# Attention on one core: sums from spare columns, reciprocals two steps later, projections as fp32r splits, TensorE's loop written out

## The reference, cut to what matters

```python
q = (x @ Wq + bq).reshape(B, N, H, d).transpose(0, 2, 1, 3)
k = (x @ Wk + bk).reshape(B, N, H, d).transpose(0, 2, 1, 3)
v = (x @ Wv + bv).reshape(B, N, H, d).transpose(0, 2, 1, 3)
scores = jnp.einsum('bhqd,bhkd->bhqk', q, k) * SCALE
allowed = jnp.abs(idx[:, None] - idx[None, :]) <= half        # half = 64
attn = jax.nn.softmax(jnp.where(allowed, scores, -jnp.inf), axis=-1)
out = jnp.einsum('bhqk,bhkd->bhqd', attn, v)
return out.transpose(0, 2, 1, 3).reshape(B, N, D) @ Wo + bo
...
h = h + attention(layernorm(h))
```

## Time and profile before

| | us |
|---|---|
| median of 3 runs (lowest, highest) | 2761.98 (2761.46, 2766.01) |
| profiled execution, its own time | 2763.8 |
| its span | 2762.1 |
| attention phase, by the windows | about 415 to 1160 |
| TensorE busy over the span | 2544.0 (92%) |
| DVE busy over the span | 1870.7 (68%) |
| mean granted TensorE clock | 0.953 |

### The profile page before, as it was taken

One profiled execution on the slowest core, in us unless ns is written; L12 is line 12 of the kernel. 1 busy time (PEld: TensorE's weight loads), 2 busy tenths in 40 slices (PEclk: granted clock), 3 DMA queues, 4 the chain that ended last, 5 costly groups with the idle time before them and its releaser, 6 DMA issues.

```text
span 2762.1 us, 52306 instructions
## 1 busy us (share of the span) xinstructions
PE 2544.0 (92%) x21673; PEld 2308.9 (84%) x21673; DVE 1870.7 (68%) x2148; ACT 1354.8 (49%) x1292; POOL 242.1 (9%) x147
## 2 busy tenths in 40 slices
PE   8959985898889889559999999999999999999999
PEld 6736684776667667459999999999999999999999
DVE  7849913655556566386766767666877777777774
ACT  2238801322223223255353443537977777777771
POOL 2202201000000000031121212100000000000000
PEclk9989996988989999879999999999999999999999
DMA  3435513000000000000000000003000000000000
GB/s 113 128 90 148 139 33 136 10 17 9 17 9 17 14 12 13 14 12 24 17 27 23 17 23 17 23 28 115 28 20 23 24 20 21 25 20 20 27 16 9
DMA packets 83907, 103.44 MB, mean 37 GB/s; under 512 B 8919, under 2 KB 75111, under 8 KB 83047
## 3 DMA queue, kind: packets, MB, share of 16 engines
q1 hardware_dynamic: 80167, 90.99, 10.9%
q0 software_dynamic: 3616, 10.54, 1.5%
HBM read 71.14 MB, written 30.36 MB: 37 GB/s over the span
## 4 chain that ended last, share of the span: by engine, by line
PE 56%; DVE 1%; issue 0%; DMA 0%; POOL 0%; ACT 0%; SPq 0%; POOLq 0%; DVEq 0%
PE spline_acc L1620 31%; PE spline_acc L1603 8%; PE spline_acc L1602 8%; PE spline_acc L1604 8%; PE spline_xT L1583 0%; DMA spline_x<-h_scr 0%; DVE spline_weights_low L1327 0%; DVE spline_xn L569 0%; DVE spline_f L1360 0%; DVE spline_t L1348 0%; DVE spline_b L1343 0%; DVE spline_b L1337 0%; DVE spline_a L1332 0%; POOL spline_rstd L1299 0%; ACT spline_a L1491 0%
## 5 line engine op out<-in xcount | busy, mean ns | idle before, releaser
L1620 PE MATMUL spline_acc<-spline_weights,spline_f 128*128 128x192 f32 x5248 | 853.0, 326 | 0.0
L1620 PEld LDWEIGHTS spline_acc<-spline_weights,spline_f 128*128 128x128 f32 x5248 | 852.8, 190 | 0.0
L1368 DVE SCALAR_TENSOR_TENSOR spline_f<-spline_n,spline_b 128x2048 f32<-128x2048 f32 x164 | 376.0, 2293 | 183.7 <-PE spline_acc L1620 181.9
L1602 PE MATMUL spline_acc<-spline_f,spline_weights_high 128*128 128x328 f32 x1536 | 479.8, 312 | 7.2 <-DVE spline_f L1360 7.2
L1603 PE MATMUL spline_acc<-spline_f,spline_weights_high 128*128 128x328 f32 x1536 | 482.4, 314 | 0.0
L1604 PE MATMUL spline_acc<-spline_f,spline_weights_low 128*128 128x328 f32 x1536 | 476.2, 310 | 0.0
L1602 PEld LDWEIGHTS spline_acc<-spline_f,spline_weights_high 128*128 128x128 f32 x1536 | 289.9, 189 | 7.4 <-issue 7.4
L1603 PEld LDWEIGHTS spline_acc<-spline_f,spline_weights_high 128*128 128x128 f32 x1536 | 289.1, 188 | 0.0
L1604 PEld LDWEIGHTS spline_acc<-spline_f,spline_weights_low 128*128 128x128 f32 x1536 | 288.7, 188 | 0.0
L1360 DVE SCALAR_TENSOR_TENSOR spline_f<-spline_n,spline_a 128x984 fp32r<-128x984 f32 x128 | 151.1, 1180 | 200.1 <-PE spline_acc L1604 198.4
L912 ACT ACTIVATE attend_probs<-scores_by_key 82x1968 f32<-82x1968 f32 x64 | 115.7, 1807 | 316.2 <-PE scores_by_key L1040 316.2
(11 more groups left out here) (154 smaller groups left out, 3567.3 us busy)
## 6 DMA issues: line engine op xcount, KB each, us to landing
sample_pos<-pos_scr SPq DMA_DIRECT2D x32, 540.0 KB, 4.4
hid_scr<-spline_hid SPq DMA_DIRECT2D x64, 164.0 KB, 1.8
spline_xn<-hid_scr SPq DMA_DIRECT2D x41, 256.0 KB, 3.1
pix_scr<-stem_by_pixel SPq DMA_DIRECT2D x32, 225.0 KB, 2.5
sample_h<-pix_scr POOLq DMA_DIRECT2D x32, 225.0 KB, 4.4
spline_weights_raw<-w SPq DMA_DIRECT2D x1, 6144.0 KB, 22.0
spline_weights<-w SPq DMA_DIRECT2D x4, 1536.0 KB, 6.1
h_scr<-attend_h SPq DMA_DIRECT2D x16, 246.0 KB
```

What stands on the lines that cost most here:

```text
L1368: nc.vector.scalar_tensor_tensor(f2[i][:], n_[u][:], MAGIC + i, b_[u][:], ALU.is_equal, ALU.mult).then_inc(f_ready, 1)
L1602: nc.tensor.matmul(z, high, x_high, start=start, stop=False)
L1620: last = nc.tensor.matmul(z, f2[i][:, r * P:(r + 1) * P], w2[:, i, r, :], start=(i == 0 and r == 0), stop=(i == 3 and r == 4 * CH - 1))
```

## The change

The edits, in the order of the diff:

1. The ones of the sums move into `va`: its spare columns 16 to 31 of each head are set to 1.0, so one `mix` gives results and sums. The second pass against `ones` is gone. The step's output is copied to SBUF by ACT (`mix_out`, to `mixed[i]`).
2. The sums (rows 16, 48, 80, 112) go to DRAM, come back as 48x41, are inverted by DVE in the step after (`invert`, behind part q = 2 of the maxima), go to DRAM again and come back broadcast to 32 rows each, in four DMAs. DVE weighs at the start of the second step after (`weigh`), and `project_out` takes the image of two steps back. SP does nothing else.
3. Loads of x and stores of h move from SP to POOL, and the residual is loaded from DRAM instead of computed from x; `bo` enters through a sum row of `wo`.
4. q, k and v are each five fp32r matmuls where there were two float32 ones: x is split by ACT (`turned`, three copies) and DVE (`low_x`), the weights once at the start.
5. Window pieces and masks are fp32r instead of bf16, with even widths.
6. Values are copied out of PSUM by ACT instead of DVE.
7. TensorE's order: in the second step `mix` is in two parts, one behind `values` and one behind part q = 3; in the first step the k projections come last. `project_out` moves from behind part 1 to behind part 0.
8. TensorE's loop is written out; the other engines keep theirs.

```diff
-            def load(t, u):
-                sp.dma_start(even[0:VIS], vis[:, b, :]).then_inc(x_in[u], 16)
...
+            def invert(t, i):
+                sp.wait_ge(mix_ready, 2 * t + i + 1)
+                sp.dma_start(total_scr[i], mixed[i][DH:P:32, :]).then_inc(total_out[i], 16)
+                sp.wait_ge(total_out[i], 16 * t + 16)
+                sp.dma_start(total[i][0:SUMS, :], total_scr[i].rearrange("j (k n) -> (j k) n", n=PART)
+                             ).then_inc(total_in[i], 16)
+                sp.wait_ge(inverted, 2 * t + i + 1)
+                sp.dma_start(rec_scr[i].rearrange("j (k n) -> (j k) n", n=PART), rec[i][0:SUMS, :]
+                             ).then_inc(rec_out[i], 16)
+                sp.wait_ge(rec_out[i], 16 * t + 16)
+                for j in range(4):
+                    sp.dma_start(spread[i][32 * j:32 * j + 32, :],
...
+            def pair(tt, u, more=True):
                 t = 2 * tt + u
                 pool.wait_ge(ln, LN_STEPS * t + LN_VAR)
                 pool.tensor_tensor(rstd[0:ROWS, :], ve[0:ROWS, :], minus_half[0:ROWS, :], ALU.pow).then_inc(pow_done, 1)
                 if not (isinstance(tt, int) and tt == 0):
-                    pool.wait_ge(h_ready, 2 * t - 2)
-                pool.tensor_tensor(resid[u][0:ROWS], x[u][0:ROWS],
-                                   bo[0:ROWS, :, :].to_broadcast([ROWS, 4, D]), ALU.add).then_inc(resid_ready, 1)
+                    leave(t - 2, u)
+                load(pool, resid[u], resid_in[u], t)
+                if more:
+                    pool.wait_ge(xn_ready, t + 1)
+                    load(pool, x[u], x_in[u], t + 2)
...
+                    if not first:
+                        weigh(t - 1, i)
                     for q in range(4):
                         if i == 0 or more:
                             maximum(nxt, q)
+                        if q == 0:
+                            if i == 0 and more:
+                                for j in range(2):
+                                    low_x(t + 1, j, use(t, X[j]))
+                            if not first:
+                                residual(tt - 1 if u == 0 else tt, v, i, use(t, Y[i]))
+                            if i == 1 and more2:
+                                norm_in(tt + 1, u)
+                        if q == 1 and i == 1 and more2:
+                            norm_out(tt + 1, u, use(t, X[1]))
...
-                nc.tensor.matmul(xb[:, bank, 0:PT], w[0:D0, 0, g, :], xT[0:D0, 0, :], start=True, stop=False)
-                nc.tensor.matmul(xb[:, bank, 0:PT], w[0:D1 + 1, 1, g, :], xT[0:D1 + 1, 1, :],
-                                 start=False, stop=True).then_inc(filled[bank], 1)
+                nc.tensor.matmul(y, high[:, 0, c], xh[:], start=True, stop=False)
+                nc.tensor.matmul(y, high[:, 0, c], xl[:], start=False, stop=False)
+                nc.tensor.matmul(y, low[:, 0, c], xh[:], start=False, stop=False)
+                nc.tensor.matmul(y, high[:, 1, c], xr[:], start=False, stop=False)
+                nc.tensor.matmul(y, low[0:D1 + 2, 1, c], xe[0:D1 + 2, :], start=False,
+                                 stop=True).then_inc(filled[bank], 1)
...
-            with pe.Fori(1, PAIRS // 2 - 1) as tt:
+            for tt in range(1, PAIRS // 2 - 1):
                 for u in range(2):
                     pair(tt, u)
```

More of the change, by code:

```diff
@@ L870, in _ @@
                 low_k(0, g, start(START["K"][g]), HG + g + 1)
-            for i in range(2):
-                values(0, i, start(START["V"][i]))
             for q in range(4):
@@ L913, in expo, with pair @@
                                      ACT.Exp, scale=SCALE).then_inc(exped, 1)
-            def pair(tt, u, more=True):
+            def pair(tt, u, first=False, more=True):
                 t = 2 * tt + u
@@ L941, in _ @@
                 high(k1[0][:, g, :], start(START["K"][g]))
+            act.wait_ge(zeros_set, 5)
+            for i in range(2):
+                values(0, i, start(START["V"][i]))
             high(mh[:], start(START["MAX"]))
-            for u in range(2):
-                pair(0, u)
+            pair(0, 0, first=True)
+            pair(0, 1)
             with act.Fori(1, PAIRS // 2 - 1) as tt:
@@ L1097, in pair @@
-                        if q == 2 and more:
+                        if q == 0:
+                            if i == 0 and more:
+                                for j in range(2):
+                                    turn_x(t + 1, j, use(t, X[j]))
+                            if not first:
+                                project_out(a - 2, i, use(t, Y[i]))
+                        if q == 2:
                             if i == 0:
-                                read(use(t, X[0]), use(t, X[1]))
-                                for g in range(2):
-                                    project(wq, g, use(t, Q[g]))
-                            else:
-                                values(0, use(t, V[0]))
@@ L1104, in pair @@
-                    if i == 0 and more:
-                        project(wq, 2, use(t, Q[2]))
-                    pe.wait_ge(exped, 2 * a + 2)
-                    mix(u, i, use(t, SUM[i]), True)
+                                if more:
+                                    read(use(t, X[0]), use(t, X[1]))
+                                    for g in range(2):
+                                        project(wqh, wql, g, use(t, Q[g]))
+                            else:
+                                if more:
+                                    values(0, use(t, V[0]))
+                                mix(a, u, i, 0, use(t, MIX[i]))
@@ new lines, in pair @@
+                    if i == 0:
+                        if more:
+                            project(wqh, wql, 2, use(t, Q[2]))
+                        read(*(start(START["V"][j]) if first else use(t - 1, V[j]) for j in range(2)))
+                        for c in range(2):
+                            mix(a, u, i, c, use(t, MIX[i]))
+                    else:
+                        mix(a, u, i, 1, use(t, MIX[i]))
+                        if more:
+                            values(1, use(t, V[1]))
@@ L1108, in pair @@
                     if nxt:
                         turn_max(a + 1, use(t, MAX[i]))
-                    if more:
-                        if i == 0:
-                            for g in range(HG):
-                                project(wk, g, use(t, K_[g]))
-                        else:
-                            values(1, use(t, V[1]))
-                    if i == 0:
-                        read(*(start(START["V"][j]) if first else use(t - 1, V[j]) for j in range(2)))
-                    mix(u, i, use(t, MIX[i]), False)
+                    if i == 0 and more:
+                        for g in range(HG):
+                            project(wkh, wkl, g, use(t, K_[g]))
```

326 lines of the change are left out of this document (178 added, 148 removed).

## The result

The changed kernel takes 2850.7 us (median of 4 runs, 2848.9 to 2854.3) against 2761.7 for the kernel before (4 runs, 2754.8 to 2766.0): ratio 1.0326, 95% interval 1.0302 to 1.0350. It is 89 us slower where 22 faster was forecast, and outside the range.

The account below looks back on a forecast made before the run. TensorE was taken to set the pace; twelve pairs at 44.1 - 43.0 gave 13.2 us, with 3.5, 2.4, -2.3, 13.3 and -6.3 a sum of 23.8: 2763.8 - 23.8 = 2740.0 us, range 2645 to 2797.

Parts of the forecast that it names:

- What goes: Attention savings: a 1.8 us mix per step, projections 0.74 for 1.21 us, values 0.9, loop return 7.3, DVE reciprocals, SP's loads.
- The k wait: First step's end: with k projections last, the next step's scores wait the full 1.3 us for the last k.
- The loop's return: TensorE's loop in attention: writing it out saves 48.0 - 40.7 = 7.3 us, in five or six pairs.
- The second step: Second step of a pair: 12.4 us of work, part 2 of queries waits 1.6, part 3 waits 0.5, 14.5 in all.
- The wait for POOL: DVE waits for POOL's power behind seven DMA issues: 7y - 1.9 us, a stall of 3.4 per pair, ends 1.8 and 7.2.
- y: One DMA issue on POOL in attention, taken at 0.75 us from earlier rows of 0.53 to 1.30.
- the slow rival: POOL becomes the bound: each 0.1 us per issue costs 9 us in all; at 1.30 the result is 2790; chance 0.25.
- The clock after the stall: TensorE at half clock behind the DVE wait: 4.0 us, ends 1.6 in all and 8; second step's drop another 1.6.
- The round trip of the reciprocals: DMAs between DVE's reciprocal and weighing, about 5 us, costed at nothing; bound 3 us per landing, 2.9 us late per pair.
- the quick rival: POOL issues at 0.53 us: stall 1.8, clock holds, 5.6 us less per pair, 2667 us; chance 0.30.
- late reciprocals: Rival: landings take 3 us, DVE weighs 2.9 us late per pair, pair 38 us, 2778; chance 0.05.
- The ends: Outside the twelve pairs: gains 3.5 and 2.4 ahead; after, -2.3, 13.3 from last half pairs, -6.3 at the end.

Follow-up runs that it names:

- the waits gone: Changed kernel with all loads and stores on SP and transfers cut to 80 and 2 rows, TensorE's loop kept: 2724.0 us, 37.5 more than written out.
- rows split: Transfers cut to 80 and 2, 32 and 14, 32 and 4 rows: changed kernel with loads and stores on SP 2686.5 us, changed kernel itself 2817.4 us.
- the norm earlier: Changed kernel with loads and stores on SP, transfers cut to 80 and 2 rows, and DVE's norm_in ahead of the second step's first maximum: 2639.9 us.
- the power first: Changed kernel with POOL computing a pair's power before issuing the seven DMAs, not behind them: 2836.8 us, ratio 1.0260.
- the corner without either cause: Changed kernel with POOL's power ahead of its DMAs and transfers cut to 80 and 2, 32 and 14, 32 and 4 rows: 2719.4 us.

## Why the prediction was wrong

**Where the miss lies.** The profiled execution took 2848.9 us where 2740.0 was forecast. Of these 109 us, 63 lie in the twelve pairs (48.3 us each for 43.0), 22 ahead of them and 24 behind them.

**What goes: nearly right.** Five fp32r matmuls of a projection take 0.86 us where 0.74 was forecast: those behind the first follow at 0.15 us, as rows 1 gave, but the first takes 0.26 (timeline of PE, changed kernel; the next group starts at 826.83):

```profile
825.97 0.42 PE L1039 MATMUL attend_spare<-attend_x_high,attend_wk_high 128*128 128x328 f32 x1 [0.48 <-ACT attend_mixed L954]
826.23 0.31 PE L1040 MATMUL attend_spare<-attend_x_low,attend_wk_high 128*128 128x328 f32 x1
...
826.83 0.40 PE L1039 MATMUL attend_spare<-attend_x_high,attend_wk_high 128*128 128x328 f32 x1
...
830.19 0.70 PE L1093 MATMUL scores_by_key<-attend_q,attend_k 32*82 32x164 f32 x24 [1.11 <-issue]
```

The k wait is the last row, 1.1 us for 1.3. The loop's return was worth what rows 2 said, in the kernel before (39) and with the waits gone (37.5); where another wait held the pair it was worth 25. A pair without the stall and at full clock was forecast at 34.0 us; with rows split, such a pair (721.6 to 757.1, granted clock 1.00) takes 35.5. The 1.5 us too little lie mostly in the projections (0.1 each) and in `project_out`, which waits 2.27 us there for its bank where I took 1.2. That the twelve pairs with the norm earlier average 35.6, the forecast's 34.0 + 1.6, is luck: their wait of part 2 is nearly gone, which the forecast had in it, and their mean clock is 0.92. The second step had the right wait in it (part 2 behind the norm, 1.6; measured 1.76).

**The wait for POOL: right mechanism, one issue mis-sized.** y, one issue on POOL, was taken at 0.75 and is 1.19 in the mean; 7y - 1.9 would then give 6.4, and DVE's wait is 7.1. The rows from which y came span it (0.53 to 1.30), but I took the value of one short-row transfer for seven that move 72 to 328 rows. The row of 0.53 was not undisturbed either, as the prediction has it: a DVE operation of 3.16 us (L414, from 192.55) runs over it. The figure of about 1 us in the Trainium skill, "DMA: Bandwidth & Descriptors", section "Latency and other measured facts", lay nearer to the measured 1.19 than mine. By the slow rival's own formula 1.19 gives 2740 + 7 x 0.44 x 13 = 2780. That is still 71 us short.

**The clock after the stall: too small.** I took 4.0 + 1.6 us with an upper end of 8. The stall is 6.45 us on TensorE, not 4, and the clock stays at 0.50 from 793 to 814: 7.0 us. From part 2 of the queries at 790.71 to that of the next pair at 838.16 TensorE waits 10.45 us in all, where the pair at full clock above waits 5.92 (it has no wait ahead of part 3, but 2.27 instead of 0.52 for `low_x`). So this pair comes out as 35.5 + 4.5 + 7.0 = 47.0, of 47.5 measured; the mean of the twelve is 48.3.

**The round trip of the reciprocals at nothing: the step that failed.** Landings were taken from rows 8, of other phases, and the bound was 3 us; `rec_scr` takes 5.0 us beside the loads (6.5 with the power first). In this kernel that is partly hidden by the stall for POOL (2.05 us of waiting at 809.51 in the pair shown), which is why the forecast's own suspect looked like the whole answer. It still costs 33 us here, 20 of them in the twelve pairs (559.8 us with rows split for 579.5), though DVE's wait for the power is longer with rows split. And it carries as much as POOL does: had y been 0.53, I estimate that the quick rival would have got not 2667 but something near 2837, the power-first kernel, in which DVE hardly waits for the power. I gave late reciprocals 0.05, and named them in the last line as what would make the forecast wrong. In the power-first kernel they do, by 117 us against the corner without either cause.

**The ends.** To the fourth power the forecast gained 5.9 us and the changed kernel loses 15.9. The first power alone comes 8.5 us later (439.43 for 430.90; with rows split 432.43), and in the fourth period DVE already waits 7.33 us for the power, which the sum left out. From the sixteenth power on, the forecast gained 4.7 us (-2.3 + 13.3 - 6.3); the changed kernel loses 19.2. The last three `project_out` that wait are these (timeline of PE):

```profile
1186.17 4.11 PE L1135 MATMUL attend_spare<-attend_wo,attend_oT 128*82 128x192 f32 x12 [6.95 <-DVE attend_oT L839]
...
1219.56 3.84 PE L1135 MATMUL attend_spare<-attend_wo,attend_oT 128*82 128x192 f32 x12 [8.64 <-DVE attend_oT L839]
1230.27 3.62 PE L1135 MATMUL attend_spare<-attend_wo,attend_oT 128*82 128x192 f32 x12 [6.86 <-DVE attend_oT L839]
```

I had one such wait, at the very end. With rows split this stretch gains 7.8 us (89.1 for 96.9), and the start, to the fourth power, 7.9 where 5.9 were forecast. That kernel has its moves on SP, so this shows that the two ends can be had, not that each piece was sized rightly.

**Open.** How the rows of a transfer are dealt to the 16 DMA engines isn't in the profile; that 82 rows land in 11 us and 80 in 2.6 is shown, and the busy share of 0.13 points to two engines, but no other cut of 82 (41 + 41, 64 + 18) was tried. Whether 46 and 36 rows are slow by themselves is not shown either: they were always in flight behind the store of h, and loads of 2 rows there took up to 5.5 us in the median. Nor was it tried why the moves on POOL cost 33 us more than on SP when the power is first and the rows are split.

## What to carry to other kernels

A small DMA on the path costs what it costs beside the transfers that are in flight with it: look up what else is moving at that moment and in how many rows, and a count like 82 is a suspect (80 + 2 landed four times faster). When DMAs are put on POOL, each blocks it (0.5 to 1.9 us here), so nothing that another engine waits for may stand behind them. Two waits in the same step hide each other, so an experiment that removes one of them and gains little does not clear it; remove both.

## What the runs showed of the hardware that I had not expected

- 246 KB in 328 rows of 768 bytes: 11.3 us to landing as 82x4 rows, 2.7 for 240 KB as 80x4 (the 2x4 beside it, 2.4). 123 KB as 82x2: 11.0; 120 KB as 80x2: 2.5.
- On SP's queue the long transfers block the issues too: with whole rows three of a pair's eight issues take 2.7 to 3.8 us each (total_scr above 3.03); with split rows most take 0.24 to 0.51 and the longest 1.35.
- POOL's issue went by the shape and not by the rows alone: 36x2 rows 0.63, 82x2 1.52, 82x4 1.87, but 80x2 0.63. Split, none of the loads took less than 0.53, so 14 issues were as long in sum as 7.
- Moving 1.9 us of DVE work, and with it a wait of TensorE of 1.76 us once per pair, raised the mean granted clock of the twelve pairs from 0.87 to 0.92 and took 46.6 us off the kernel.
